# A small-tile feed-forward tail on one core: rounding moved from GpSimd to ScalarE, and the VectorE queue reordered

## The chip, the cores and the metric

One core of a Trainium2 chip runs the kernel. The metric is the device time of one execution in microseconds (us); the median of several is compared. Five queues run side by side and meet only in semaphores: TensorE (PE), VectorE (DVE), ScalarE (ACT), GpSimd (POOL) and SyncE (SP), which here only starts transfers.

## The reference

One layer over x of 16 x 64 rows of 256: cross-attention on a context, a state-space block (Mamba), and a quantised feed-forward block, which the change is about. Cut to that block:

```python
def _act_quant(x):
    scale = 127.0 / jnp.clip(jnp.max(jnp.abs(x), axis=-1, keepdims=True), 1e-05)
    return jnp.clip(jnp.round(x * scale), -128.0, 127.0) / scale
def _bitlinear(x, w):
    return jnp.einsum('bsi,oi->bso', _act_quant(x), _weight_quant(w))
gate = jax.nn.silu(_bitlinear(xn, w_gate))      # 256 -> 1024
up = _bitlinear(xn, w_up)
x = x + _bitlinear(gate * up, w_down)           # 1024 -> 256, xn = layernorm(x)
```

## The kernel before

The 1024 rows are 8 tiles of 128 rows. Three stages follow one another: attention (to about 190 us), the scan of the state-space block (to about 360 us), and the feed-forward tail. Each engine has one queue, written out by hand; an instruction waits for semaphores (`wait_ge`) and whatever stands behind it waits too.

**The scan** is cut into 64 halves `hu`. For each, PE writes the inflow into PSUM, DVE scans it (`scan`, L1601, into a ring of 4 buffers), POOL multiplies by C (`weigh`, L1897, `g_ready`), and PE turns and adds it (`accumulate`, L759). `weigh(hu)` needs `scan(hu)`, and `scan(hu)` needs `weigh(hu - 4)`. Between the halves stand pieces of the tail for the first tiles: on DVE the statistics (`ffn_statistics`, L1659 and L1662, after halves 50, 52, 60 and 61) and the scale of a row (`input_scale`: reduce L1675, L1677, reciprocal L1679, and for the tiles 0 to 2 also L1681, which writes two scales for gate and up; after halves 54 and 56, and for tile 2 behind the last scan); on POOL `offset_input` (L1912, L1914, L1921) after halves 48, 50 and 60, and `rounded_to_bf16` (L1938) after halves 54 and 56.

**The tail**, for each tile t: normalise the row (ACT L1123 for tiles 0 to 2, POOL L1932 else), largest magnitude and its inverse (`input_scale`), scale and round by adding a large number (ACT L1130 or POOL L1965, `hi`), subtract it again and write bf16 (POOL L1938, `input_to_bf16`, `f_hq`), transpose on PE (L790), copy to SBUF (ACT L1221, `copy_input`), gate and up matmuls (L801, L812), SiLU (ACT L1302), product in DVE (`product`, L1688), its largest magnitude (`largest`, L1693), `inner_scale` (L1705, L1707, L1709), scale and round (ACT L1309, `round_inner`), back to bf16 (DVE L1716, `inner_to_bf16`), transpose (L824), copy (ACT L1317, `copy_inner`), down matmul (L837), output (DVE L1724), store. Only tile 7 does the inner part in two halves.

The second half of the state-space output, tiles 4 to 7, is still being made while tiles 0 to 3 are in the tail: `gate(7)` (DVE L1610) needs the last `accumulate`; then PE turns four blocks (L770), ACT copies them (`copy_yz`, L1215), PE multiplies them (`out_proj_of`, L778) and DVE adds them to the residual (`add_scan(1, 0)` and `add_scan(1, 1)`, L1649), after which the statistics of tiles 4, 5 and 6, 7 can be taken. The order of the DVE queue in the middle of the tail is

```python
product(2); largest(2); inner_scale(2); inner_to_bf16(1)
add_scan(1, 0); ffn_statistics(4); ffn_statistics(5); inner_to_bf16(2); input_scale(4); product(3)
```

and that of ACT there is `round_inner(1)`, `round_inner(2)`, `copy_input(3, 4)`, `copy_yz(1, 2, 2)`, `copy_inner(0)`, `silu_gate(3)`. PE has after `out_proj_of(1, 1, 3)`: `turn_input(3, 4)`, `turn_gated(1, 2, 2)`, `activations(0)`, `gates(3)`, `turn_gated(1, 3, 2)`, `up(3)`, `activations(1)`, then `out_proj_of` for the last two tiles.

Of the kernel before, what the change touches and what calls it, by code (L numbers as in the profile page):

```python
# [17 lines left out]
ALU = mybir.AluOpType  # L18
# [6 lines left out]
P = 128  # L25
# [4 lines left out]
NT = B * L // P  # L30
# [76 lines left out]
def build(nc, x, ctx_t, mask, wq, wkv, wproj, bproj, vecs, cons, win, wall, wout, wg, wu, wd, out):  # L107
    with ExitStack() as ctx:
# [106 lines left out]
        f_s2 = [sb(f"f_s2{t}", [P, 5]) for t in range(NT)]  # L215
        f_nmean = sb("f_nmean", [P, NT_ACT])
        C_M2, C_CL2, C_INV2, C_A, C_OUT = range(5)

# [109 lines left out]
        f_inv, f_sgs = sem("f_inv", DVE), sem("f_sgs", DVE)  # L328
        f_hi_ready, f_hq = sem("f_hi_ready", POOL), sem("f_hq", POOL)
# [4 lines left out]
        f_a, f_os, f_gi_ready = sem("f_a", DVE), sem("f_os", POOL), sem("f_gi_ready", ACTE)  # L334
        f_gq, f_gqt, f_gqt_sb = sem("f_gq", DVE), sem("f_gqt", PE), sem("f_gqt_sb", ACTE)
        f_down, f_out = sem("f_down", PE), sem("f_out", DVE)
        stored = [sem("stored0", SP), sem("stored1", SP)]
# [142 lines left out]
        def _(pe):  # L480
# [346 lines left out]
            def down(t):  # L827

                if t == 0:
                    pe.wait_ge(yz_sb, count(NG * GT))  # L830
                if t == 3:
                    pe.wait_ge(x2_ready, count(NT))
                pe.wait_ge(f_out, count(t if t < 3 else t - 1))
                for n, cols in enumerate(inner_parts(t)):
                    pe.wait_ge(f_gqt_sb, count(t + 1 + n))
# [153 lines left out]
        def _(act):  # L989
# [216 lines left out]
            def copy_yz(g, tt, k):  # L1206
# [8 lines left out]
                act.activation(yz[:, tt % 2], bank(k), ACT.Copy).then_inc(yz_sb, 1)  # L1215

            def copy_input(t, k):
# [71 lines left out]
            round_input(0)  # L1289
            slot(15)  # L1290
            round_input(1)
            copy_input(0, SPARE_BANK)
            copy_input(1, SPARE_BANK)
            normal_input(2)
# [9 lines left out]
            def round_inner(t):  # L1304

                act.wait_ge(f_a, count(t + 1))
                act.wait_ge(f_gq, count(t - 1))
                for cols in inner_parts(t):
                    act.activation(f_gi[t % 2][:, cols], f_gu[t % 2][:, cols], ACT.Copy,  # L1309
                                   scale=f_s2[t][:, C_A:C_A + 1], bias=MAGIC).then_inc(f_gi_ready, 1)  # L1310

            def copy_inner(t):

                act.wait_ge(f_down, count(t - 1))
                for n, cols in enumerate(inner_parts(t)):
# [9 lines left out]
            silu_gate(1)  # L1325
            round_inner(0)
# [10 lines left out]
            copy_yz(1, 3, 2)  # L1337
            copy_inner(1)
            round_inner(3)
            copy_input(4, 4)  # L1340
            silu_gate(4)
            copy_inner(2)
            copy_input(5, 4)
            copy_inner(3)
            silu_gate(5)
            round_inner(4)
            copy_input(6, 4)
            silu_gate(6)
            round_inner(5)
# [11 lines left out]
        def _(dve):  # L1361
# [334 lines left out]
            def inner_scale(t):  # L1696

                s2, up_scale = f_s2[t], f_s[t][:, C_SU:C_SU + 1]

                def col(c):  # L1700
                    return s2[:, c:c + 1]

                dve.wait_ge(f_max2, count(t + 1))
                dve.wait_ge(*weights_scaled(t))
                dve.tensor_scalar(col(C_CL2), col(C_M2), up_scale, EPS, ALU.mult, ALU.max).then_inc(f_cl2, 1)  # L1705
                dve.wait_ge(f_cl2, count(t + 1))
                dve.reciprocal(col(C_INV2), col(C_CL2)).then_inc(f_inv2, 1)  # L1707
                dve.wait_ge(f_inv2, count(t + 1))
# [112 lines left out]
        def _(pool):  # L1821
# [112 lines left out]

            def input_to_bf16(t):

                pool.wait_ge(f_hqt, count(t - 1))
                pool.tensor_scalar(f_hqb[t % 2], f_hi[t % 2], MAGIC, 127.0, ALU.subtract, ALU.min).then_inc(f_hq, 1)  # L1938

            def scale_weights_of(t):  # L1940
# [6 lines left out]
            def scale_output(t):  # L1947

                s2 = f_s2[t]
                pool.wait_ge(f_cl2, count(t + 1))  # L1950
                pool.tensor_scalar(s2[:, C_OUT:C_OUT + 1], s2[:, C_CL2:C_CL2 + 1], wmean[:, 2:3], 1.0 / 127.0, ALU.mult,
                                   ALU.mult).then_inc(f_os, 1)

            def rounded_to_bf16(t):

                if t == 0:
                    pool.wait_ge(delta_ready, count(NG * NC))
                pool.wait_ge(f_hi_act, count(t + 1))
                input_to_bf16(t)

            def round_input(t):

                pool.wait_ge(f_inv, count(t + 1))
                pool.wait_ge(f_hq, count(t - 1))
                pool.tensor_scalar(f_hi[t % 2], f_h[t % 2], f_s[t][:, C_INV:C_INV + 1], MAGIC, ALU.mult, ALU.add  # L1965
                                   ).then_inc(f_hi_ready, 1)
                pool.wait_ge(f_hi_ready, count(t - NT_ACT + 1))
                input_to_bf16(t)

# [14 lines left out]
            for hu in range(NHU - 1):  # L1984
# [25 lines left out]
            scale_weights_of(5)  # L2010
            scale_output(3)
            normal_input(6)
            normal_input(7)
            round_input(6)
            scale_weights_of(6)
# [62 lines left out]
```

## Time and profile before

| what | value |
|---|---|
| median of 3 runs | 410.5 us (409.54 to 410.86) |
| profiled execution, its own time | 412.68 us |
| its span, first to last instruction | 410.8 us |
| busy share of the span: PE, DVE, ACT, POOL | 88%, 85%, 68%, 69% |
| mean granted TensorE clock | 0.992 |

The page gives the busy time of each engine, the chain of work that ended last, and groups of instructions by line. Some 1.9 us of the profiled execution lie outside its span. The tail, which the change touches, is the stretch from about 340 us on.

### The profile page before, as it was taken

How to read it: one execution, taken by the hardware profiler on the slowest of the kernel's cores; microseconds unless marked ns; L12 is line 12 of the kernel's file. 1: busy time of each engine (PE TensorE's matmuls, PEld its weight loads, DVE VectorE, ACT ScalarE, POOL GpSimd, SP SyncE). 2: the span in 40 equal slices, each digit the busy share in tenths (PEclk: the TensorE clock that was granted, in tenths of full speed). 3: DMA queues.
4: the chain of work that ended last, by engine and by line, in shares of the span. 5: the costliest groups of instructions: out<-in, count | busy, mean ns of one | idle time of the engine just before them, and what ended most of it. 6: DMA issues, size and time to landing. Idle time of an engine off the chain costs nothing.

```text
span 410.8 us, 8698 instructions
## 1 busy us (share of the span) xinstructions
PE 361.4 (88%) x2886; PEld 246.2 (60%) x2886; DVE 348.2 (85%) x723; ACT 278.7 (68%) x596; POOL 285.5 (69%) x333
## 2 busy tenths in 40 slices
PE   7899999999998999887798999898889778889774
PEld 5556767676776765453465566566576656557442
DVE  1558888797989778958989999989999999988795
ACT  1267589769966993489569879857874554266574
POOL 0056475565657472248999999999999699986830
PEclk9999999999999999999699999999999999999999
DMA  7981010110100000019400001364000000000001
GB/s 209 357 360 53 2 51 14 42 51 3 53 2 0 2 3 0 2 38 249 128 2 0 2 4 26 92 191 129 2 1 2 1 2 0 2 0 2 14 26 65
DMA packets 23039, 22.41 MB, mean 55 GB/s; under 512 B 1074, under 2 KB 20914, under 8 KB 22484
## 3 DMA queue, kind: packets, MB, share of 16 engines
q1 hardware_dynamic: 22436, 21.39, 16.7%
q8 instruction: 23, 0.38, 0.4%
q10 hardware_dynamic: 560, 0.48, 0.4%
q14 instruction: 20, 0.16, 0.1%
HBM read 20.75 MB, written 1.12 MB: 53 GB/s over the span
## 4 chain that ended last, share of the span: by engine, by line
PE 28%; DVE 20%; ACT 17%; POOL 17%; issue 16%; DMA 1%; DVEq 0%; PEld 0%; POOLq 0%; SPq 0%; ACTq 0%; PEldq 0%
POOL both L1897 12%; PE ps L544 7%; ACT both L1181 5%; DVE both L1601 4%; PE ps L513 4%; PE ps L496 3%; DVE both L1425 2%; PE ps L531 2%; PE ps L607 2%; PE ps L574 2%; ACT both L1016 2%; PE ps L759 2%; PE ps L561 2%; DVE f_s L1693 1%; ACT both L1167 1%
## 5 line engine op out<-in xcount | busy, mean ns | idle before, releaser
L1897 POOL TENSOR_TENSOR both<-both 128x1024 f32<-128x1024 f32 x64 | 150.4, 2386 | 2.4 <-DVE both L1601 1.8
L1601 DVE TENSOR_TENSOR_SCAN both<-both,ps 128x1024 f32<-128x1024 f32 x64 | 143.0, 2271 | 5.6 <-PE ps L749 5.5
L1843 POOL TENSOR_SCALAR both<-both,rden 128x256 f32<-128x256 f32 x128 | 61.7, 497 | 62.8 <-DVE rden L1432 62.6
L1181 ACT ACTIVATE both<-delta,a_neg 128x504 f32<-128x504 f32 x120 | 74.8, 704 | 12.3 <-DVE both L1601 12.2
L759 PE MATMUL ps<-con,both 128*128 128x128 f32 x512 | 72.5, 281 | 7.5 <-POOL both L1897 7.4
L759 PEld LDWEIGHTS ps<-con,both 128*128 128x128 f32 x512 | 56.8, 142 | 29.5 <-issue 16.3
L1016 ACT ACTIVATE both<-both,negmax 128x256 f32<-128x256 f32 x128 | 63.3, 498 | 15.7 <-DVE negmax L1425 15.7
L749 PE MATMUL ps<-both 32*128 32x256 f32 x512 | 46.7, 435 | 11.7 <-DVE both L1601 9.6
L1425 DVE CUSTOM_DVE_ANT_0 both<-ps,both 128x256 f32<-128x256 f32 x128 | 46.9, 417 | 6.7 <-PE ps L496 5.5
L513 PEld LDWEIGHTS ps<-con,both 128*128 128x128 f32 x256 | 30.6, 141 | 12.7 <-issue 8.0
L513 PE MATMUL ps<-con,both 128*128 128x128 f32 x256 | 38.2, 275 | 0.0
L749 PEld LDWEIGHTS ps<-both 32*128 32x128 f32 x512 | 20.5, 186 | 27.6 <-DVE both L1601 15.5
L544 PE MATMUL ps<-both 128*128 128x512 f32 x64 | 33.0, 640 | 2.7 <-DMA both<-in_wkv 1.3
L574 PE MATMUL ps<-both 128*128 128x256 f32 x128 | 31.1, 387 | 0.5 <-DVE both L1400 0.5
L1437 DVE COPY both<-ps 128x512 f32<-128x512 f32 x32 | 21.6, 676 | 10.2 <-PE ps L513 10.2
L1022 ACT ACTIVATE both<-ps 128x512 f32<-128x512 f32 x32 | 18.8, 588 | 14.6 <-PE ps L513 14.6
L574 PEld LDWEIGHTS ps<-both 128*128 128x128 f32 x128 | 23.1, 190 | 6.0 <-issue 2.7
L1016 ACT ACTIVATION_READ_ACCUMULATOR both<-both,negmax 128x1 f32 x128 | 24.5, 191 | 0.0
L1826 POOL TENSOR_TENSOR vareps<-meanvar,eps 128x1 f32<-128x1 f32 x24 | 6.3, 261 | 25.5 <-DVE meanvar L1377 25.5
L496 PE MATMUL ps<-both 32*128 32x256 f32 x256 | 20.6, 399 | 3.0 <-DVE negmax L1425 2.0
L544 PEld LDWEIGHTS ps<-both 128*128 128x128 f32 x64 | 11.3, 197 | 14.9 <-issue 13.0
L496 PEld LDWEIGHTS ps<-both 32*128 32x128 f32 x256 | 13.2, 184 | 8.3 <-issue 6.7
(151 smaller groups left out, 616.7 us busy)
## 6 DMA issues: line engine op xcount, KB each, us to landing
both<-bounce SPq DMA_DIRECT2D x16, 512.0 KB, 6.4
both<-in_ctx_t SPq DMA_DIRECT2D x8, 512.0 KB, 3.4
both<-in_wg SPq DMA_DIRECT2D x1, 1024.0 KB, 8.9
both<-in_wu SPq DMA_DIRECT2D x1, 1024.0 KB, 10.6
both<-in_wd SPq DMA_DIRECT2D x1, 1024.0 KB, 12.6
win_sb<-in_win SPq DMA_DIRECT2D x1, 1024.0 KB, 13.8
resid<-in_x SPq DMA_DIRECT2D x1, 896.0 KB, 6.3
both<-in_wkv SPq DMA_DIRECT2D x2, 256.0 KB, 3.4
```

What stands on the lines that cost most here:

```text
L496: mm = pe.matmul(score_bank(tile, v)[:, bb * LK:(bb + 1) * LK], q2[rows, tile.par, hf, bb].rearrange("p r q -> p (r q)"), kt_sb[rows, tile ...
L513: tr = pe.transpose(pt_bank(tile, u)[:, (q * 2 + kt) * P:(q * 2 + kt + 1) * P], sm[:, u, q * LK + kt * P:q * LK + (kt + 1) * P], ident)
L544: mm = pe.matmul(kv_bank(tile, hf), wkv_sb[:, k, hf * P:(hf + 1) * P], ctx_sb[:, tile.par, k], start=k == 0, stop=k == KD - 1)
L574: mm = pe.matmul(kv_bank(tile, 1 - bb)[:, kt * D:(kt + 1) * D], ctx_sb[:, tile.par, k, bb * LK + kt * P:bb * LK + (kt + 1) * P], wkv_sb[:, ...
L749: mm = pe.matmul(bank(inflow_bank(hu) + sq).rearrange("p (n h t) -> p n h t", n=HN, h=2)[:, :, th], ut[rows, e.idx % 2, tt], bd[rows, e.nh ...
L759: mm = pe.matmul(bank(Y_BANK)[:, e.tt * P:(e.tt + 1) * P], g_sb[:, hu % RING_G, n * P:(n + 1) * P], ident, start=False, stop=e.nh == NH - ...
L1016: act.activation(s, s, ACT.Exp, scale=-1.0, bias=negmax[:, u, q:q + 1], accum_out=den[:, u, q:q + 1]).then_inc(expd, 1)
L1181: act.activation(da[sl % 2].rearrange("p (a s n t) -> p a s n t", a=GT, n=HN, s=2)[:, :, :, n, 1:L], delta[:, idx % RING_D].rearrange("p ( ...
L1425: dve.tensor_tensor_reduce(sm[:, u, q * LK:(q + 1) * LK], score_bank(tile, u)[:, q * LK:(q + 1) * LK], maskf[:, tile.par, q * LK:(q + 1) * ...
L1601: dve.tensor_tensor_scan(h_sb[:, hu % RING_H], da[e.slot % 2][:, e.tt * HU:(e.tt + 1) * HU], bank(inflow_bank(hu), 2), 0.0, ALU.mult, ALU. ...
L1843: pool.tensor_scalar(s, s, rden[:, u, q:q + 1], 1.0, ALU.mult, ALU.mult).then_inc(normed, 1)
L1897: pool.tensor_tensor(g_sb[:, hu % RING_G].rearrange("p (n s t) -> p s n t", n=HN, s=2), h_sb[:, hu % RING_H].rearrange("p (s n t) -> p s n ...
```

## The change

Six edits. (1) `input_to_bf16` goes from POOL (subtract and minimum in one operation) to ACT (an activation that adds minus the large number), placed in ACT's queue by hand, the first one in the middle of the last block of decays. With that `rounded_to_bf16` leaves POOL. (2) `product` multiplies by the up scale too (`scalar_tensor_tensor` in place of `tensor_tensor`), so that `inner_scale` needs two small operations and no longer L1709. (3) A one-column SiLU on ACT stands ahead of the first real one, so that the table is loaded there. (4) In the DVE queue `add_scan(1, 0)` and the statistics of 4 and 5 stand ahead of `inner_scale(2)` and `inner_to_bf16(1)`; `input_scale(4)` stands ahead of `inner_to_bf16(2)`; the statistics of 7 ahead of `inner_to_bf16(3)` and `output(0)`. On POOL `scale_output(3)` stands behind two normalisations. (5) At the end `largest(7)` and `inner_scale(7)` stand ahead of `inner_to_bf16(6)`, that of 7 ahead of `output(5)`, and on ACT `round_inner(7)` ahead of `copy_inner(6)`. (6) The second half of the last `copy_inner` is made by DVE (`copy_last_half`).

```diff
+            def input_to_bf16(t):
+                if t < NT_ACT:
+                    act.wait_ge(f_hi_act, count(t + 1))
+                else:
+                    act.wait_ge(f_hi_ready, count(t - NT_ACT + 1))
+                act.wait_ge(f_hqt, count(t - 1))
+                act.activation(f_hqb[t % 2], f_hi[t % 2], ACT.Copy, bias=-MAGIC).then_inc(f_hq, 1)
...
-            slot(15)
+            half_slot(15, 0)
+            input_to_bf16(0)
+            half_slot(15, 1)
             round_input(1)
             copy_input(0, SPARE_BANK)
+            input_to_bf16(1)
             copy_input(1, SPARE_BANK)
             normal_input(2)
...
+            act.activation(f_warm[:], eps[:], ACT.Silu).then_inc(passed, 1)
             act.wait_ge(y_seed, count(NG * NC))
...
             round_inner(1)
+            input_to_bf16(3)
             round_inner(2)
...
+            round_inner(7)
             copy_inner(6)
-            round_inner(7)
             copy_inner(7)
...
-                dve.tensor_tensor(f_gu[t % 2], bank(0, 2), f_sg[t % 2], ALU.mult).then_inc(f_gu_ready, 1)
+                dve.wait_ge(*weights_scaled(t))
+                dve.scalar_tensor_tensor(f_gu[t % 2], bank(0, 2), f_s[t][:, C_SU:C_SU + 1], f_sg[t % 2], ALU.mult, ALU.mult
+                                         ).then_inc(f_gu_ready, 1)
...
-                dve.tensor_scalar(col(C_A), col(C_INV2), up_scale, 127.0, ALU.mult, ALU.mult).then_inc(f_a, 1)
...
+            def copy_last_half():
+                t = NT - 1
+                cols = inner_parts(t)[1]
+                dve.wait_ge(f_gqt, count(t + 2))
+                dve.wait_ge(f_down, count(t - 1))
+                dve.tensor_copy(f_gqtb[t % 2].rearrange("p k t -> p (k t)")[:, cols], f_inner(1)[:, cols]
+                                ).then_inc(f_last_half, 1)
...
             largest(2)
-            inner_scale(2)
-            inner_to_bf16(1)
             add_scan(1, 0)
             ffn_statistics(4)
             ffn_statistics(5)
+            inner_scale(2)
+            inner_to_bf16(1)
+            input_scale(4)
             inner_to_bf16(2)
-            input_scale(4)
             product(3)
...
             ffn_statistics(6)
+            ffn_statistics(7)
             inner_to_bf16(3)
             output(0)
-            ffn_statistics(7)
...
             product(7)
-            inner_to_bf16(6)
             largest(7)
             inner_scale(7)
+            inner_to_bf16(6)
             output(4)
+            inner_to_bf16(7)
             output(5)
-            inner_to_bf16(7)
+            copy_last_half()
...
-                if hu in (54, 56):
-                    rounded_to_bf16((54, 56).index(hu))
             weigh(NHU - 1)
-            rounded_to_bf16(2)
```

## Rows read from the trace of the kernel before

**Rows 1.** The chain that ended last, in order of time: start us, us, what.

```profile
360.04 4.69 POOL both L1897 x2
364.77 1.10 PE ps L759 x8
...
385.76 1.23 POOL xnt L1932
```

**Rows 2.** Timeline of POOL, end of the scan: start us, us, engine, line, operation.

```profile
330.89 9.30 POOL L1897 TENSOR_TENSOR both<-both 128x1024 f32<-128x1024 f32 x4
340.28 1.07 POOL L1938 TENSOR_SCALAR dtb<-xnt 128x256 bf16<-128x256 f32 x1
357.74 6.98 POOL L1897 TENSOR_TENSOR both<-both 128x1024 f32<-128x1024 f32 x3
```

**Rows 3.** Timeline of DVE, end of the scan and start of the tail.

```profile
334.12 1.47 DVE L1681 TENSOR_SCALAR f_s<-wmean,f_s 128x2 f32<-128x2 f32 x1
340.56 0.21 DVE L1681 TENSOR_SCALAR f_s<-wmean,f_s 128x2 f32<-128x2 f32 x1
348.47 2.28 DVE L1601 TENSOR_TENSOR_SCAN both<-both,ps 128x1024 f32<-128x1024 f32 x1
354.22 4.46 DVE L1601 TENSOR_TENSOR_SCAN both<-both,ps 128x1024 f32<-128x1024 f32 x2
359.30 0.81 DVE L1681 TENSOR_SCALAR f_s<-wmean,f_s 128x2 f32<-128x2 f32 x1
361.22 1.23 DVE L1688 TENSOR_TENSOR zst<-ps,xc 128x1024 f32<-128x1024 f32 x1 [1.11 <-ACT xc L1302]
366.51 1.21 DVE L1693 TENSOR_REDUCE f_s<-zst 128x1 f32<-128x1024 f32 x1
```

**Rows 4.** Line L1622, its two forms: durations min/median/max in ns.

```profile
L1622 DVE TENSOR_TENSOR u_sb<-xc,delta x4: 661/686/1710, 182.1 to 198.0; 128x512 f32<-128x512 f32 x4
L1622 DVE TENSOR_TENSOR u_sb<-ps,delta x4: 662/665/665, 266.4 to 319.8; 128x512 f32<-128x512 f32 x4
```

**Rows 5.** Timeline of DVE, middle of the tail.

```profile
373.36 0.75 DVE L1649 TENSOR_TENSOR resid<-ps,resid 128x256 f32<-128x256 f32 x2
378.18 1.23 DVE L1688 TENSOR_TENSOR zst<-ps,xc 128x1024 f32<-128x1024 f32 x1
387.01 0.42 DVE L1675 TENSOR_REDUCE f_s<-xnt 128x1 f32<-128x256 f32 x1 [1.94 <-POOL xnt L1932]
400.01 1.22 DVE L1688 TENSOR_TENSOR zst<-ps,xc 128x1024 f32<-128x1024 f32 x1
```

**Rows 6.** Groups by line and shape: busy us, mean ns, idle before.

```profile
L1716 DVE TENSOR_SCALAR both<-delta 128x1024 bf16<-128x1024 f32 x7 | 4.8, 687 | 0.0
L1938 POOL TENSOR_SCALAR dtb<-xnt 128x256 bf16<-128x256 f32 x6 | 6.9, 1147 | 0.5
L1709 DVE TENSOR_SCALAR f_s<-f_s 128x1 f32<-128x1 f32 x8 | 1.7, 214 | 0.3
L1130 ACT ACTIVATE xnt<-xnt,f_s 128x256 f32<-128x256 f32 x1 | 0.5, 497 | 0.0
L1557 DVE SCALAR_TENSOR_TENSOR xc<-ps,vec,xc 128x496 f32<-128x496 f32 x4 | 2.9, 720 | 1.6 <-ACT zst L1114 1.6
```

**Rows 7.** Timeline of ACT, start, middle and end of the tail.

```profile
358.78 1.28 ACT L1302 ACT_TABLE_LOAD   x1 [0.37 <-PE ps L801]
372.88 1.15 ACT L1309 ACTIVATE delta<-zst,f_s 128x1024 f32<-128x1024 f32 x1 [1.98 <-DVE f_s L1709]
406.37 1.08 ACT L1317 ACTIVATE both<-ps 128x512 bf16<-128x512 bf16 x2 [0.55 <-PE ps L824]
```

**Rows 8.** Timeline of PE, middle of the tail.

```profile
369.41 3.62 PE L778 MATMUL ps<-wout_sb,yz 128*128 128x256 f32 x16
374.36 1.04 PE L801 MATMUL ps<-wgq,dtb 128*128 128x512 bf16 x4 [0.33 <-ACT dtb L1221]
```

**Rows 9.** The last output, timeline of DVE.

```profile
408.18 0.48 DVE L1724 SCALAR_TENSOR_TENSOR z<-ps,f_s,resid 128x256 f32<-128x256 f32 x1 [1.51 <-PE ps L837]
```

More of the change, by code:

```diff
@@ L216, in build @@
         f_nmean = sb("f_nmean", [P, NT_ACT])
+        f_warm = sb("f_warm", [P, 1])
         C_M2, C_CL2, C_INV2, C_A, C_OUT = range(5)
@@ L328, in build @@
         f_inv, f_sgs = sem("f_inv", DVE), sem("f_sgs", DVE)
-        f_hi_ready, f_hq = sem("f_hi_ready", POOL), sem("f_hq", POOL)
+        f_hi_ready, f_hq = sem("f_hi_ready", POOL), sem("f_hq", ACTE)
         f_hqt, f_hqt_sb = sem("f_hqt", PE), sem("f_hqt_sb", ACTE)
@@ L333, in build @@
         f_gu_ready, f_cl2, f_inv2 = sem("f_gu_ready", DVE), sem("f_cl2", DVE), sem("f_inv2", DVE)
-        f_a, f_os, f_gi_ready = sem("f_a", DVE), sem("f_os", POOL), sem("f_gi_ready", ACTE)
+        f_os, f_gi_ready = sem("f_os", POOL), sem("f_gi_ready", ACTE)
         f_gq, f_gqt, f_gqt_sb = sem("f_gq", DVE), sem("f_gqt", PE), sem("f_gqt_sb", ACTE)
+        f_last_half = sem("f_last_half", DVE)
         f_down, f_out = sem("f_down", PE), sem("f_out", DVE)
@@ L834, in down @@
                 for n, cols in enumerate(inner_parts(t)):
-                    pe.wait_ge(f_gqt_sb, count(t + 1 + n))
+                    if n:
+                        pe.wait_ge(f_last_half, count(1))
+                    else:
+                        pe.wait_ge(f_gqt_sb, count(t + 1))
                     for j in range(cols.start // P, cols.stop // P):
@@ L1215, in copy_yz @@
                 act.activation(yz[:, tt % 2], bank(k), ACT.Copy).then_inc(yz_sb, 1)
+            def input_to_bf16(t):
+                if t < NT_ACT:
+                    act.wait_ge(f_hi_act, count(t + 1))
+                else:
+                    act.wait_ge(f_hi_ready, count(t - NT_ACT + 1))
+                act.wait_ge(f_hqt, count(t - 1))
+                act.activation(f_hqb[t % 2], f_hi[t % 2], ACT.Copy, bias=-MAGIC).then_inc(f_hq, 1)
             def copy_input(t, k):
@@ L1304, in round_inner @@
             def round_inner(t):
-                act.wait_ge(f_a, count(t + 1))
+                act.wait_ge(f_inv2, count(t + 1))
                 act.wait_ge(f_gq, count(t - 1))
@@ L1309, in round_inner @@
                     act.activation(f_gi[t % 2][:, cols], f_gu[t % 2][:, cols], ACT.Copy,
-                                   scale=f_s2[t][:, C_A:C_A + 1], bias=MAGIC).then_inc(f_gi_ready, 1)
+                                   scale=f_s2[t][:, C_INV2:C_INV2 + 1], bias=MAGIC).then_inc(f_gi_ready, 1)
             def copy_inner(t):
                 act.wait_ge(f_down, count(t - 1))
-                for n, cols in enumerate(inner_parts(t)):
+                for n, cols in enumerate(inner_parts(t)[0:1]):
                     act.wait_ge(f_gqt, count(t + 1 + n))
@@ L1325, in _ @@
             silu_gate(1)
+            input_to_bf16(2)
             round_inner(0)
@@ L1338, in _ @@
             copy_inner(1)
+            input_to_bf16(4)
             round_inner(3)
             copy_input(4, 4)
+            input_to_bf16(5)
             silu_gate(4)
@@ L1345, in _ @@
             silu_gate(5)
+            input_to_bf16(6)
             round_inner(4)
             copy_input(6, 4)
+            input_to_bf16(7)
             silu_gate(6)
@@ L1696, in inner_scale @@
             def inner_scale(t):
-                s2, up_scale = f_s2[t], f_s[t][:, C_SU:C_SU + 1]
-                def col(c):
-                    return s2[:, c:c + 1]
+                s2 = f_s2[t]
                 dve.wait_ge(f_max2, count(t + 1))
-                dve.wait_ge(*weights_scaled(t))
-                dve.tensor_scalar(col(C_CL2), col(C_M2), up_scale, EPS, ALU.mult, ALU.max).then_inc(f_cl2, 1)
+                dve.tensor_scalar(s2[:, C_CL2:C_CL2 + 1], s2[:, C_M2:C_M2 + 1], EPS, 1.0 / 127.0, ALU.max, ALU.mult
+                                  ).then_inc(f_cl2, 1)
                 dve.wait_ge(f_cl2, count(t + 1))
-                dve.reciprocal(col(C_INV2), col(C_CL2)).then_inc(f_inv2, 1)
-                dve.wait_ge(f_inv2, count(t + 1))
-                dve.tensor_scalar(col(C_A), col(C_INV2), up_scale, 127.0, ALU.mult, ALU.mult).then_inc(f_a, 1)
+                dve.reciprocal(s2[:, C_INV2:C_INV2 + 1], s2[:, C_CL2:C_CL2 + 1]).then_inc(f_inv2, 1)
             def inner_to_bf16(t):
@@ L1933, in normal_input @@
                                    ALU.mult).then_inc(f_xn, 1)
-            def input_to_bf16(t):
-                pool.wait_ge(f_hqt, count(t - 1))
-                pool.tensor_scalar(f_hqb[t % 2], f_hi[t % 2], MAGIC, 127.0, ALU.subtract, ALU.min).then_inc(f_hq, 1)
             def scale_weights_of(t):
@@ L1950, in scale_output @@
                 pool.wait_ge(f_cl2, count(t + 1))
-                pool.tensor_scalar(s2[:, C_OUT:C_OUT + 1], s2[:, C_CL2:C_CL2 + 1], wmean[:, 2:3], 1.0 / 127.0, ALU.mult,
+                pool.tensor_scalar(s2[:, C_OUT:C_OUT + 1], s2[:, C_CL2:C_CL2 + 1], wmean[:, 2:3], 1.0, ALU.mult,
                                    ALU.mult).then_inc(f_os, 1)
[L1954 to L1959, printed above, removed]
             def round_input(t):
@@ L1966, in round_input @@
                                    ).then_inc(f_hi_ready, 1)
-                pool.wait_ge(f_hi_ready, count(t - NT_ACT + 1))
-                input_to_bf16(t)
             pool.wait_ge(s_ready, count(NT * 8))
@@ L2010, in _ @@
             scale_weights_of(5)
-            scale_output(3)
             normal_input(6)
             normal_input(7)
+            scale_output(3)
             round_input(6)
```

## The prediction

> **What bounds the kernel now.** I read the page first: DVE is busy for 85% of the span, PE for 88%, POOL for 69%, so no share alone decides, and the change touches nothing before 340 us. So I read the chain of waits from there on. Up to 364.7 us it is POOL, one multiplication after the other; then PE turns the last one, and from there the chain runs through DVE, with POOL's normalisations between them [rows 1]. The timelines say how tight each queue is. POOL runs its 64 multiplications at 9.30 / 4 = 2.33 us each, and at 340.28 one conversion to bf16 of 1.07 us stands between them [rows 2]. DVE is just as full: none of its rows up to 360.11 has idle time before it, and a scan takes 2.28 us [rows 3]. Both engines set the pace, so time taken from POOL shows only where DVE does not need it itself.
>
> The row to look at longest is L1681, two columns wide. It took 1.47, 0.21 and 0.81 us [rows 3]. The long ones end at 335.59 and 360.11; POOL's multiplications end at 330.89 + 2 x 2.325 = 335.54 and at 357.74 + 2.33 = 360.07 [rows 2]. The short one ran inside POOL's bf16 conversion (340.28 to 341.35). So L1681 waits for the end of a two-input POOL multiplication that is already running, and not for the conversion. L1622 says the same from another side: with both inputs in SBUF one of four took 1710 ns against a median of 686, with one in PSUM all four took 662 to 665 [rows 4]. One-column operations (L1677, L1709 at 214 ns) show no such wait [rows 6].
>
> **Part by part: the end of the scan.** The change takes the conversion out of POOL at 340.28. The next multiplication then starts there and runs to 342.61. L1681 of tile 1 comes at 340.56, which is now inside it. It ends some 0.05 us behind it as in the two long cases, at 342.65 instead of 340.77: DVE +1.9 us, and with it every scan from there. This phase is no accident of one run: the first L1681 waited for POOL's end at 335.54 and so tied DVE to POOL; two scans, the reduce and two small ones later DVE is at 340.56, and two multiplications later POOL is at 340.2.
>
> POOL, relieved of 2 x 1.15 us, now waits for DVE. Before, scan 60 ended at 348.47 + 2.28 = 350.75 [rows 3]; now at 352.6. Multiplication 60 follows at once; three of them and the 1.15 us of `offset_input` later, number 63 starts at 352.65 + 3 x 2.33 + 1.15 = 360.8 and ends at 363.1 (before: 357.74 + 6.98 = 364.72 [rows 2]). From scan 60's end to L1681 of tile 2 it took 359.30 - 350.75 = 8.55 us, so it now comes at 361.15, again inside a multiplication, and ends at 363.15. The product of tile 0 starts there. Before it started at 361.22, held for 1.11 us by SiLU [rows 3], whose wait is gone now, since the gates need only multiplication 60. So the tail starts 1.9 us late on DVE although POOL ends 1.6 us early.
>
> The Trainium skill (SBUF — State Buffer, Who interferes with whom) calls the port pair that VectorE and GpSimd share an exclusive lock, held for a whole instruction, that a two-port `tensor_scalar` or a two-input VectorE operation needs. The two long L1681 and the long L1622 agree; that the one at 340.56 ran through a POOL conversion in 0.21 us does not.
>
> **Product and scales.** `scalar_tensor_tensor` is not in the trace at this size: with PSUM and 496 columns it took 720 ns, and scaled by the product's slope (1.23 us at 1024) a 1024-column one lies between 1.23 (no extra) and 1.49 us (720 x 1024 / 496). I take 1.29: most of the 720 is fixed and per-column time, and the product's own row is nearest in size. L1709 goes: 0.22 us of DVE from one start to the next. Net -0.16 us for each tile, bounds -0.22 and +0.04. From product(0) to largest(1) DVE took 5.29 us before, of which PE's wait was a part; now 2.89 for tile 0, 1.20 and 0.60 for product(1) and `gate(7)`, 4.7 in all: largest(1) at 367.8, +1.3 against 366.51 [rows 3].
>
> **The middle.** `add_scan(1, 0)` needs the first two output projections. They ended at 369.41 + 3.62 = 373.03 [rows 8]; they hang on `gate(7)`, also 1.3 us late (ready 367.9, not 366.6), so they end at 374.1 to 374.3. DVE gets there at 373.3 (product(2) +1.1) and waits; behind it stand two adds (0.7) and two statistics (1.2), and only then `inner_scale(2)`, done at 376.5. Before, ACT's `round_inner(2)` started at 372.88 [rows 7]; now at 376.5, +3.6. On ACT `copy_input(3)` stands behind it, for it wait the gates of tile 3 (374.36 before [rows 8], about 378.0 now), and behind them in PE's queue the fourth turn, up(3), and the last two projections. Not all of it arrives: before, product(3) at 378.18 [rows 5] was itself held by POOL's normalisation of tile 4; now SiLU(3) holds it to 380.4, +2.2. `add_scan(1, 1)` is also 2.2 late. Here POOL's relief pays: before, two conversions and three small operations stood ahead of `normal_input(6)` (385.76 [rows 1]); now POOL is free when the statistics come. The reduce of tile 6 was held 1.94 us by it, to 387.01 [rows 5]; I get 388.2 and product(4) at 389.1, +1.3 to +1.5. Were the old order of these lines kept, gates(3) would come at 375.3, and the end about 1.7 us sooner. So this reorder costs 1.7, and what it should bring, early statistics, is bounded by the projections, which it makes late itself.
>
> The moved conversions cost ACT about 0.4 each (256 columns with a pointer scale took 497 ns [rows 6]; bounds 0.4 to 0.5) and they lie in ACT's waits, 1.98 us at one place alone [rows 7]; 0.6 each would move nothing, and if that cover went it would be 0.4 us a tile. The early table load puts 1.28 us [rows 7] ahead of gates that now end earlier; DVE is at L1681 until 363.15, so it is worth nothing either way here (up to -1.1 if DVE were early). `scale_output(3)` and the statistics of 7: nothing, output(0) is not waited for before down(3).
>
> **Tiles 4 to 7.** From product(4) on DVE has no idle time until product(7) at 400.01 [rows 5]. Three tiles at -0.16 give -0.5: +0.9 there.
>
> **The end.** From product(7) to the last output it took 8.17 us [rows 5, 9]. The largest magnitude and its scale now come first, so bf16(6) starts 2.9 us behind product(7) and not 1.1. After it: 0.69, then turn 6 (0.6), copy 6 (1.0), down 6, half a turn of tile 7, half a copy (0.6), the last down. With the waits between them that is 5.9, 8.8 in all: +0.6. DVE's copy of the second half saves ACT about half of 1.08 us [rows 7], but DVE makes it beside the first half and down needs the first; whether it takes 0.42 or 0.68 the end stands.
>
> **Sum.** +1.9 (two port waits, SiLU's wait gone) - 0.6 (product(0) to largest(1)) + 0.9 (middle: +1.3 to +2.2) - 0.8 (POOL free for tile 6) - 0.5 (three tiles) + 0.6 (end) = +1.5 us, on a span of 410.8 and a profiled time of 412.68. The median lies 2.2 below that profiled one; I carry the difference over: 410.5 + 1.5 = 412.0. Worked through queue by queue with these durations the kernel before comes out 0.5 us short at product(7); with as much again for the steps that no row shows, +0.7 to +2.3 is this case's own range: 411.2 to 412.8.
>
> **The rivals.** What a measurement of this kernel can tell from no change is about 0.3%, 1.2 us.
>
> *The port waits do not come* (faster). If L1681 finds POOL between two instructions or the conversion on ACT changes their phase, nothing is lost at 340.56 and 361.15. Product(0) then starts at 359.3 (multiplication 60 ends at 353.1, and behind it lie one turn, the gates, a table load and SiLU, 4.5 us in all), and is 1.9 early instead of 1.9 late; the middle gives back 1.7, the rest brings what is said above: -2.6, 407.9 us. For it speaks that L1681 at 340.56 would meet POOL only 0.3 us behind an instruction's start; against it the three rows and the fixed phase. It decides as soon as L1681 of tile 1 takes under 0.6 us and that of tile 2 as well. Chance 0.2.
>
> *Only one of the two comes* (about no change). With the first gone POOL is 1.8 us ahead of DVE and number 63 starts at 358.95, so L1681 at 359.30 waits to 361.3: the same product(0) as before, -0.3 in all. With the second gone, -0.8. 409.7 to 410.2 us. Chance 0.18.
>
> *The queues slip further* (slower still). If `scalar_tensor_tensor` costs 1.49 and DVE, the fullest engine, waits for a late POOL at tile 6 as before, it is 5 x 0.2 + 0.8 more: 413.8 us. Chance 0.1.
>
> My forecast, both waits and the late middle: 0.52.
>
> **How the numbers follow.** The forecast's range is split by +1.2 us: a third of it lies below. Slower: two thirds of 0.52 and 0.1, 0.44. Same: one third of 0.52 and most of 0.18, 0.32. Faster: 0.2 and a rest of the middle case, 0.24. The range leaves out half of the fast case and most of the slowest: 408.0 to 413.2.
>
> **What would show it.** In the profile of the changed kernel L1681's successor should have one instance of about 2.1 us at 340.6 and another of 2.0 at 361.1; product(0) at 363.1; DVE idle before `add_scan(1, 0)` for 0.8; ACT idle before `round_inner(2)` for some 4 us; gates(3) at 378; 8.8 us from product(7) to the last output. I am wrong if the two L1681 are short, if gates(3) come before 376, or if the product with its scale takes much over 1.3 us.

## The result

The changed kernel takes 417.9 us (median of 4 runs, 417.6 to 418.7); the kernel before took 410.7 (4 runs, 409.5 to 412.8). The ratio is 1.0173, with a 95% interval of 1.014 to 1.0206: 7.2 us slower. The forecast was 412.0 us in a range of 408.0 to 413.2, so its sign holds and its size does not. The profiled execution took 417.61 us with a span of 415.8, and the mean granted clock of TensorE is 0.975, where it was 0.992.

**The two port waits came.** The timeline of DVE in the changed kernel, L1705 being what L1681 was (start us, us, engine, line, operation, and in brackets the idle time before it with its releaser):

```profile
338.66 1.99 DVE L1705 TENSOR_SCALAR f_s<-wmean,f_s 128x2 f32<-128x2 f32 x1
...
359.17 1.99 DVE L1705 TENSOR_SCALAR f_s<-wmean,f_s 128x2 f32<-128x2 f32 x1
361.08 1.27 DVE L1713 SCALAR_TENSOR_TENSOR zst<-ps,f_s,xc 128x1024 f32<-128x1024 f32 x1
...
372.81 0.76 DVE L1673 TENSOR_TENSOR resid<-ps,resid 128x256 f32<-128x256 f32 x2 [1.30 <-PE ps L780]
...
381.15 1.28 DVE L1713 SCALAR_TENSOR_TENSOR zst<-ps,f_s,xc 128x1024 f32<-128x1024 f32 x1 [2.88 <-PE ps L814]
...
402.39 1.27 DVE L1713 SCALAR_TENSOR_TENSOR zst<-ps,f_s,xc 128x1024 f32<-128x1024 f32 x1
...
410.89 0.43 DVE L1745 COPY both<-ps 128x512 bf16<-128x512 bf16 x1 [3.37 <-PE ps L826]
...
413.17 0.48 DVE L1753 SCALAR_TENSOR_TENSOR z<-ps,f_s,resid 128x256 f32<-128x256 f32 x1 [1.46 <-PE ps L842]
```

And POOL's there:

```profile
335.92 11.65 POOL L1927 TENSOR_TENSOR both<-both 128x1024 f32<-128x1024 f32 x5
347.87 2.36 POOL L1927 TENSOR_TENSOR both<-both 128x1024 f32<-128x1024 f32 x1 [0.29 <-DVE both L1625]
350.70 2.35 POOL L1927 TENSOR_TENSOR both<-both 128x1024 f32<-128x1024 f32 x1 [0.48 <-DVE both L1625]
...
354.16 6.99 POOL L1927 TENSOR_TENSOR both<-both 128x1024 f32<-128x1024 f32 x3
```

The second multiplication of the first row ends at 335.92 + 2 x 2.33 = 340.58 and L1705 at 340.65; the last one of the tail ends at 361.15 and L1705 at 361.16. Where the kernel before had 0.21 and 0.81 us [rows 3] there are now twice 1.99, and POOL, relieved of its conversions, waits for DVE (0.29 and 0.48).

**Then PE stops for 3.3 us, and comes back at half its clock.** ACT and PE in the middle and at the end:

```profile
354.86 1.28 ACT L1337 ACT_TABLE_LOAD   x1
375.13 1.15 ACT L1326 ACTIVATE delta<-zst,f_s 128x1024 f32<-128x1024 f32 x1 [4.62 <-DVE f_s L1729]
```

```profile
362.41 1.04 PE L814 MATMUL ps<-wuq,dtb 128*128 128x512 bf16 x4 [2.32 <-DVE zst L1713]
...
372.72 0.61 PE L826 MATMUL ps<-identb,both 128*128 128x128 bf16 x8
376.61 1.89 PE L803 MATMUL ps<-wgq,dtb 128*128 128x512 bf16 x4 [3.28 <-ACT dtb L1235]
378.29 1.06 PE L772 MATMUL ps<-con,zst 128*128 128x128 f32 x4
379.14 1.91 PE L814 MATMUL ps<-wuq,dtb 128*128 128x512 bf16 x4
...
404.10 1.03 PE L842 MATMUL ps<-wdq,both 128*128 128x256 bf16 x8 [1.27 <-ACT both L1334]
406.06 0.81 PE L826 MATMUL ps<-identb,both 128*128 128x128 bf16 x8 [0.94 <-DVE both L1736]
408.14 1.86 PE L842 MATMUL ps<-wdq,both 128*128 128x256 bf16 x8 [1.27 <-ACT both L1334]
...
411.27 1.87 PE L842 MATMUL ps<-wdq,both 128*128 128x256 bf16 x8 [0.41 <-ACT both L1334]
```

Windows of 2 us of the same kernel (busy time and count of PE, weight loads, DVE, ACT, POOL; then the granted clock, the DMA share and GB/s):

```profile
372.00:374.00 2.00, 1.33 (x16) 1.02 (x14) 1.09 (x3) 0.00 (x0) 0.00 (x0) 1.00 0.01 4
374.00:376.00 2.00, 0.00 (x0) 0.00 (x0) 1.50 (x6) 0.86 (x1) 1.50 (x3) 0.90 0.00 0
376.00:378.00 2.00, 1.39 (x4) 0.57 (x5) 1.08 (x4) 1.96 (x4) 1.81 (x4) 0.50 0.00 0
378.00:380.00 2.00, 2.00 (x9) 1.19 (x7) 0.27 (x1) 1.46 (x2) 2.00 (x3) 0.50 0.00 0
...
382.00:384.00 2.00, 2.00 (x9) 1.73 (x9) 1.90 (x5) 1.33 (x2) 0.00 (x0) 0.89 0.00 0
...
408.00:410.00 2.00, 1.86 (x10) 1.37 (x11) 0.00 (x0) 0.00 (x0) 0.00 (x0) 0.50 0.19 66
410.00:412.00 2.00, 1.59 (x13) 1.17 (x11) 0.82 (x2) 0.60 (x1) 0.00 (x0) 0.50 0.00 0
```

The column to read is the granted clock, 1.00 being 2.4 GHz and 0.50 being 1.2 GHz. The four gate matmuls of tile 3 took 1.04 us before [rows 8] and take 1.89 now, up(3) 1.91, and DVE waits 2.88 us for it. At the end the last two groups of down matmuls take 1.86 and 1.87 instead of 1.03. In the kernel before every such window from 366 to 410 us shows 1.00; its stretches at half clock lie between 190 and 210 us.

The table counts the us in each trace from the start of the two-column operation of tile 1 (340.56 before, 338.66 after). Absolute times would mislead: between 200 and 210 us DVE is busy for 8.04 us in the profiled run before and for 10.00 in the one after, and what lies behind is shifted by about as much. The last two columns are differences to before.

| start of | before | forecast | after |
|---|---|---|---|
| product(0) | 20.66 | +1.9 | +1.76 |
| gates(3) | 33.80 | +3.6 | +4.15 |
| product(3) | 37.62 | +2.2 | +4.87 |
| product(4) (387.76 before) | 47.20 | +1.3 to +1.5 | +4.88 |
| product(7) | 59.45 | +0.9 | +4.28 |
| last output | 67.62 | +1.5 | +6.89 |

The 6.9 us of this table are the 7.2 of the medians to 0.3. Up to gates(3) the forecast follows to 0.6 us; at product(3) the kernel is 2.7 us later than forecast, and behind product(7) it loses 2 more.

### The profile page after: what moved, and what is told of

It reads as the page before. It is cut to its first block, busy times and chain, and to the rows that moved or that the text cites. A ratio compares the mean times of both kernels' runs of the same rounds, so it can differ in the third digit from the quotient of the medians.

```text
span 415.8 us, 8688 instructions
## 1 busy us (share of the span) xinstructions
PE 365.5 (88%) x2882; PEld 248.8 (60%) x2886; DVE 349.9 (84%) x716; ACT 281.4 (68%) x604; POOL 279.1 (67%) x325
## 4 chain that ended last, share of the span: by engine, by line
PE 34%; DVE 26%; issue 14%; ACT 13%; POOL 10%; DMA 1%; DVEq 1%; PEld 0%; SPq 0%; ACTq 0%; POOLq 0%; PEldq 0%
DVE both L1625 8%; PE ps L546 7%; POOL both L1927 6%; ACT both L1186 5%; PE ps L515 4%; PE ps L498 3%; PE ps L761 2%; PE ps L533 2%; PE ps L780 2%; PE ps L751 2%; DVE both L1449 2%; PE ps L576 2%; ACT both L1021 2%; PE ps L563 2%; DVE f_s L1719 1%
## 5 line engine op out<-in xcount | busy, mean ns | idle before, releaser
L761 PE MATMUL ps<-con,both 128*128 128x128 f32 x512 | 71.2, 278 | 3.2 <-POOL both L1927 3.2
L515 PEld LDWEIGHTS ps<-con,both 128*128 128x128 f32 x256 | 30.6, 141 | 12.7 <-issue 8.0
L515 PE MATMUL ps<-con,both 128*128 128x128 f32 x256 | 38.2, 275 | 0.0
```

The costliest lines, as they stand in the source:

```text
L515: tr = pe.transpose(pt_bank(tile, u)[:, (q * 2 + kt) * P:(q * 2 + kt + 1) * P], sm[:, u, q * LK + kt * P:q * LK + (kt + 1) * P], ident)
L761: mm = pe.matmul(bank(Y_BANK)[:, e.tt * P:(e.tt + 1) * P], g_sb[:, hu % RING_G, n * P:(n + 1) * P], ident, start=False, stop=e.nh == NH - ...
```

## The experiments

Times are medians; ratios, with their 95% intervals, are to the kernel before on the same chip. Four kernels (all three, and the three parts put into the kernel before) ran on another chip than the others; the kernel before took 411.2 us there and 410.7 here, so a difference of medians across the two can be off by some 0.5 us. The ratios on record can differ from the quotient of two medians by up to 0.3%. In the expectations theory A is the account that the profile after suggests: port waits, a late middle, and a clock that falls in PE's gap; its rivals put the time elsewhere. Where matmuls are added, they write a bank that nobody reads.

**The old order in the middle of the DVE queue**, all else as after:

```diff
             largest(2)
+            inner_scale(2)
+            inner_to_bf16(1)
             add_scan(1, 0)
             ffn_statistics(4)
             ffn_statistics(5)
-            inner_scale(2)
-            inner_to_bf16(1)
-            input_scale(4)
             inner_to_bf16(2)
+            input_scale(4)
```

> The changed kernel with the old order in the middle of the DVE queue (inner_scale(2) and inner_to_bf16(1) ahead of add_scan(1, 0), inner_to_bf16(2) ahead of input_scale(4)). Theory A (the late inner_scale(2) starves PE for 3.3 us, its clock falls to half, and gates(3), up(3) and what lies between run at half speed): PE's gap ahead of gates(3) under 1.5 us, gates(3) 1.04 us and not 1.89, granted clock 1.0 from 374 to 390, 1.7 us for the order and some 3.0 us for the clock, so 413.2 us; the slow clock at the end stays. Theory B (queue order alone, the clock falls whatever the gap): 1.7 us, so 416.2, gates(3) still 1.9 us. The two port waits of 1.99 us stay in both.

411.7 us (10 runs), ratio 1.0002 (0.997 to 1.0035): the order gives back 6.2 us, more than either theory said. Gates(3) start without a gap, at full clock. But the profiled run also had a full clock at the end (8.71 us from product(7) to the last output, not 10.78), and half clock elsewhere, behind the gap ahead of up(1). In the trace this is -4.1 us between product(0) and product(7) and -2.1 behind it. The reorder alone thus did not separate the middle from the clock of the end. The window with that gap in this kernel:

```profile
358.00:364.00 6.00, 3.69 (x16) 2.37 (x15) 5.36 (x6) 2.45 (x3) 3.25 (x4) 0.72 0.00 0
```

**Two one-column scales** in place of the two-column one, all else as after:

```diff
-dve.tensor_scalar(col(C_SG, 2), wmean[:, 0:2], col(C_CL), None, ALU.mult).then_inc(f_sgs, 1)
+dve.tensor_scalar(col(C_SG), wmean[:, 0:1], col(C_CL), None, ALU.mult).then_inc(passed, 1)
+dve.tensor_scalar(col(C_SU), wmean[:, 1:2], col(C_CL), None, ALU.mult).then_inc(f_sgs, 1)
```

> The changed kernel with the two-column scaling of tiles 0 to 2 written as two one-column operations. Theory A (a two-column operation needs both ports and waits for POOL's running multiplication, a one-column one does not): no DVE operation of that line over 0.25 us, product(0) some 3.5 to 3.9 us behind nothing, that is about 1.9 us earlier each for tiles 1 and 2 less 0.2 for the added operation, limited by the gates to about 2.5; the end earlier by 2 to 3.5: 414.5 to 416. Theory B (the DVE waits were hidden behind SiLU and the projections): under 0.5 us, 417.5.

411.5 us (10 runs), ratio 1.0 (0.9976 to 1.0025): 6.4 us less than the changed kernel, again more than expected. Each one-column operation takes 0.20 us beside POOL's running multiplications, and product(0) comes 4.0 us sooner, counted from the scales of tile 0 (24.86 us against 28.87), since that tile's wait of 1.47 goes too. Product(0) to product(7) gains 1.25 and the end 0.9: PE is at half clock for less of both (up(3) takes 1.50 and not 1.91, the last two groups of down matmuls 1.32 and 1.72). The middle gap is still there:

```profile
371.15 1.87 PE L803 MATMUL ps<-wgq,dtb 128*128 128x512 bf16 x4 [2.90 <-ACT dtb L1235]
373.67 1.50 PE L814 MATMUL ps<-wuq,dtb 128*128 128x512 bf16 x4
```

**PE kept busy in the middle gap**, with all waits left in:

```diff
+def warm(t, n):
+    pe.wait_ge(f_silu, count(t))
+    for _ in range(n):
+        pe.matmul(bank(6), identb[:], wgq[:, 0, 0:512], start=True, stop=True)
...
+            warm(3, 14)
             gates(3)
```

> The changed kernel with 14 more matmuls of 512 columns into a free bank ahead of the wait of gates(3), so that PE has no gap there; nothing else is moved. Theory A (half clock because of the gap): gates(3), up(3), the turn and two thirds of the last projections run at full clock, 0.85 + 0.45 + 0.87 + 0.45 + 0.4 = 3.0 us less, 414.9 us, ACT's wait for inner_scale(2) unchanged at 4.6. Theory B (the clock is not what is lost): no change or up to 0.3 slower, 418.

413.4 us (10 runs, 412.7 to 417.5), ratio 1.0069 (1.0035 to 1.0103): 4.5 us won by adding work, 1.5 more than expected.

```profile
362.36 1.04 PE L819 MATMUL ps<-wuq,dtb 128*128 128x512 bf16 x4 [2.33 <-DVE zst L1719]
...
373.11 3.19 PE L798 MATMUL ps<-wgq,identb 128*128 128x512 bf16 x14
376.55 1.04 PE L808 MATMUL ps<-wgq,dtb 128*128 128x512 bf16 x4 [0.25 <-ACT dtb L1241]
```

Gates(3) start when they did (37.94 us behind the scales of tile 1, after: 37.95) but take 1.04, and product(3) is 2.1 us earlier, product(7) 2.8. In this run the end had full clock as well (8.71 us from product(7) to the last output), without any edit to it, which the expectation had not counted. The ten runs have mean clocks of 0.975 to 0.996, so the clock fell in more places in some of them than in this one.

**PE kept busy at the end only**: `warm(8, 4)` ahead of the down matmuls of tile 5, the activations of tile 6 and its down matmuls.

> The changed kernel with 4 more matmuls of 512 columns ahead of each of down(5), activations(6) and down(6), into a bank that SiLU(7) has left. Theory A (the clock falls at the end because PE has more and longer gaps there than before): down(6) 1.04 and not 1.86 us, down(7) 1.04 and not 1.87, turns 0.85 and not 1.06: 0.8 + 0.2 + 0.9 less, about 416.0 us. Theory B (the end is late by its queue order alone, 0.6): 417.9. Cost if the added matmuls delay the real ones: up to 0.4.

416.8 us (4 runs), ratio 1.0134 (1.0093 to 1.0175). The end takes 8.71 us and all its down matmuls 1.03, 2.1 less than after; the middle is as in after. The time falls by only 1.0, for two reasons. In the profiled run another place lost its clock, one that had it in after and in the run above, behind a gap of the same length; that costs 0.7 us by product(7):

```profile
362.39 1.86 PE L819 MATMUL ps<-wuq,dtb 128*128 128x512 bf16 x4 [2.32 <-DVE zst L1721]
...
377.40 1.89 PE L808 MATMUL ps<-wgq,dtb 128*128 128x512 bf16 x4 [3.28 <-ACT dtb L1243]
```

And two of the four runs took 3.5 and 3.6 us outside their span, from first to last instruction, where the kernels without added matmuls take 1.8 to 1.9; why is not known. The spans themselves are 413.7 to 414.4 us against 415.8 to 416.9 in the changed kernel, some 2.1 less by their medians, which is what the end gives.

**PE kept busy in all three gaps**: nine matmuls ahead of up(1), behind a wait for the last scan, then 14 and 3 x 4 as above.

> The changed kernel, its queues as they are, with added matmuls into free banks in all the long gaps of PE: 9 ahead of up(1), 14 ahead of gates(3), 4 each ahead of down(5), activations(6) and down(6). Theory A (the time above the forecast of 412.0 is TensorE's half clock and nothing else): granted clock 1.0 from 352 us on, 412 to 413 us, 5 us under the changed kernel. Theory B (half of it is something else, not seen yet): 414.5 or more.

412.7 us (12 runs, 411.0 to 415.6), ratio 1.0051 (1.0023 to 1.008). The windows and the DVE timeline:

```profile
350.00:366.00 16.00, 12.90 (x94) 8.54 (x95) 15.53 (x19) 6.71 (x10) 12.33 (x11) 1.00 0.00 0
366.00:384.00 18.00, 17.75 (x108) 12.71 (x109) 13.49 (x32) 10.91 (x16) 7.52 (x15) 1.00 0.00 1
...
398.00:412.00 14.00, 8.66 (x71) 5.39 (x69) 7.68 (x17) 5.80 (x7) 1.54 (x2) 1.00 0.13 47
```

```profile
359.10 1.99 DVE L1717 TENSOR_SCALAR f_s<-wmean,f_s 128x2 f32<-128x2 f32 x1
...
372.73 0.76 DVE L1685 TENSOR_TENSOR resid<-ps,resid 128x256 f32<-128x256 f32 x2 [1.30 <-PE ps L780]
...
399.48 1.27 DVE L1725 SCALAR_TENSOR_TENSOR zst<-ps,f_s,xc 128x1024 f32<-128x1024 f32 x1
...
408.19 0.48 DVE L1765 SCALAR_TENSOR_TENSOR z<-ps,f_s,resid 128x256 f32<-128x256 f32 x1 [0.83 <-PE ps L847]
```

Both port waits of 1.99 us and DVE's 1.30 us ahead of the first `add_scan` are still in it; only the clock differs, 1.00 throughout from 330 us to the last output. The clock therefore cost the changed kernel about 5 us: 5.1 by the medians (417.86 - 412.72), 4.9 from the scales of tile 1 to the last output in the traces, 5.3 by the medians of the spans. What lies ahead does not enter: the changed kernel's profiled run has a clock of 0.66 between 190 and 200 us and this run 1.00, and yet the scales of tile 0 start at 332.21 and 332.15. Not every run had the full clock (means of 0.987 to 1.0). This kernel is what the forecast described, and it stands 0.7 us from it; even product(3) is held by SiLU (0.77 us), as forecast, and no longer by up(3).

**The old orders of the middle and of the end**, the two-column scales kept. The end's edit is

```diff
             product(7)
+            inner_to_bf16(6)
             largest(7)
             inner_scale(7)
-            inner_to_bf16(6)
             output(4)
-            inner_to_bf16(7)
             output(5)
+            inner_to_bf16(7)
...
-            round_inner(7)
             copy_inner(6)
+            round_inner(7)
```

> The changed kernel with both old orders and the two-column scales kept, so that the port waits alone are left of the three losses. Theory A: two waits of 2.0 us, 3.7 us later than e7_all_three at product(0), 409.5, a little under the kernel before; the clock falls in some runs in the 2.3 us gap ahead of up(1), which adds up to 2 us. Theory B (with the middle mended the port waits are covered): 406.

410.3 us (12 runs), ratio 0.9989 (0.9963 to 1.0015), as expected (409.5, and up to 2 more where the clock falls). PE's gap in the middle is gone, and at the end its gaps are those of the kernel before but for 0.3 us (1.26, 1.26 and 0.38, at full clock). The port waits still leave one ahead of up(1), behind which the clock is half for part of the time:

```profile
364.13 1.43 PE L814 MATMUL ps<-wuq,dtb 128*128 128x512 bf16 x4 [2.31 <-DVE zst L1713]
```

**One-column scales and the old middle**, with the new end kept:

> The changed kernel with one-column scales and the old order in the middle, the new order at the end kept. Against e7_all_three it tells what the new end costs. Theory A: 8.7 us from product(7) to the last output against 7.9 in e7, so 405.9 and up to 1 us more where the clock falls in the longer gaps. Theory B (the end order is neutral): 405.1.

408.2 us (8 runs), ratio 0.9912 (0.9883 to 0.9941), above the 405.9 to 406.9 expected. It lies 3.0 above the next kernel, which ran on the other chip and from which it differs in the end alone; counted from the scales of tile 0 the traces differ by 2.8. Its end takes 10.68 us, at half clock:

```profile
400.00:406.00 6.00, 3.76 (x21) 2.41 (x19) 1.30 (x3) 0.60 (x1) 0.00 (x0) 0.50 0.12 44
```

The eight runs fall into two groups: five with mean clocks of 0.984 to 0.987 and spans of 406.3 to 406.9 us, three with 0.995 to 1.0 and 404.6 to 405.1. The same program thus loses some 1.7 us or not, as its clock falls or not.

**All three**: one-column scales, old middle, old end; the conversions on ACT, the scaled product, the early table and DVE's half copy stay.

> The changed kernel with all three put back or mended: one-column scales, the old order in the middle of the DVE queue, and the old order at the end (inner_to_bf16(6) ahead of largest(7), copy_inner(6) ahead of round_inner(7) on ACT). Theory A (what the change brings is real, POOL relieved and one small operation less a tile, and was covered by the three losses): product(0) 2 to 3 us earlier against the last scan than before, no idle time ahead of the first add_scan, 8.2 us from product(7) to the last output and not 8.7: 406 to 408 us, faster than before. Theory B (the gain was never there): 410.7, like before. Clock drops that come in some runs may add 1 to 2 us.

405.1 us (6 runs), ratio 0.9854 (0.9821 to 0.9887), under the 406 to 408 expected: faster than both kernels, than the one before by 6.1 us on the same chip and than the changed one by 12.7 us across chips. The granted clock is 1.00 in every window from 330 us to the last output. Its end, on DVE:

```profile
394.61 1.27 DVE L1714 SCALAR_TENSOR_TENSOR zst<-ps,f_s,xc 128x1024 f32<-128x1024 f32 x1
395.80 0.68 DVE L1737 TENSOR_SCALAR both<-delta 128x1024 bf16<-128x1024 f32 x1
...
402.49 0.48 DVE L1754 SCALAR_TENSOR_TENSOR z<-ps,f_s,resid 128x256 f32<-128x256 f32 x1 [0.59 <-PE ps L842]
```

From product(7) to the last output it takes 7.88 us; bf16(6) starts 1.2 behind product(7). At full clock the new order takes 8.71: the order itself costs 0.8 us, and the clock, where it falls, 2.0 on top.

Last, parts of the change put into the kernel before. **One-column scales alone**:

> The kernel before with the one-column scales alone. Its two waits for POOL (1.26 and 0.6 us) go. Theory A: POOL's queue sets the end of the scan there and SiLU holds product(0), so little comes of it: 410.0 to 410.7. If DVE were what binds there, 409.

411.0 us (10 runs), ratio 0.9999 (0.9973 to 1.0025). Nothing: product(0) comes 27.11 us behind the scales of tile 0, before 27.10. DVE no longer waits for POOL, but it waits longer for SiLU ahead of product(0), 1.64 us where it was 1.11 [rows 3], so its port waits had cost nothing there:

```profile
357.72 1.23 DVE L1689 TENSOR_TENSOR zst<-ps,xc 128x1024 f32<-128x1024 f32 x1 [1.64 <-ACT xc L1302]
```

**The conversions on ACT alone** (edit 1), and **that with one-column scales**:

> The kernel before with one part of the change alone: the conversions to bf16 made by ACT at the places where the change puts them; no new order on DVE, no product with scale, no early table. Theory A: two waits of 2.0 us for POOL's running multiplication on DVE, so product(0) 1.8 us later against the second scale than before, POOL's relief gives back 0.8 to 1: 411.5, plus 1 to 2 us where the clock falls in the gap of 2.3 us ahead of up(1). Theory B (POOL was the bound and is relieved of 3.4 us before the tail): 408 to 409.

> As e9_before_act_only, with one-column scales, so that DVE has no wait for POOL's multiplications. Theory A: product(0) 3.7 us earlier than in e9 against the scans, the end 3 us earlier than e9 and 2 to 3 us earlier than before: 407.5 to 408.7. Theory B (the port waits were hidden): as e9.

410.3 us (10 runs), ratio 0.9974 (0.9948 to 0.9999), and 406.8 us (4 runs), ratio 0.9899 (0.9861 to 0.9937), 0.7 under the range expected. Taking the conversions from POOL is enough to make both long waits, without any reorder:

```profile
338.56 1.99 DVE L1698 TENSOR_SCALAR f_s<-wmean,f_s 128x2 f32<-128x2 f32 x1
359.08 1.99 DVE L1698 TENSOR_SCALAR f_s<-wmean,f_s 128x2 f32<-128x2 f32 x1
```

Product(0) comes 28.87 us behind the scales of tile 0 with the waits and 24.84 without (before: 27.10). So the edit costs 1.8 us there as it was made, and brings 2.3 with one-column scales. The first kernel still came out 1.2 us lower than expected: between product(0) and product(7) it gains 1.4 us against before and at the end 0.3, where I had credited POOL's relief with 0.8. From the scales of tile 0 on this leaves it even with the kernel before (+0.1 us); the 0.9 us between the medians lie ahead of them or in the scatter. In the kernel before the one-column scales were worth nothing. Here they are worth 3.5 us, and as much in the changed kernel with the old middle (411.7 - 408.2); in the changed kernel itself 6.4, the clock included. With both old orders the medians of two chips say 5.2 (410.3 - 405.1), the traces 3.7. The prices of these edits do not add, because each one decides which wait the next one meets.

## Why the forecast was right in sign and wrong in size

**The port waits: right.** Forecast: two of 2.0 to 2.1 us and product(0) +1.9; measured 1.99, 1.99 and +1.76. That they wait for POOL's two-input multiplication follows from their ends (0.01 and 0.07 us behind POOL's) and from the one-column kernels, where nothing waits in the same places. The Trainium skill (SBUF — State Buffer, Who interferes with whom) calls the shared port pair an exclusive lock, and the rows of 1.98 to 2.00 us in seven kernels agree. That one column escapes it at 0.20 us is what these runs add.

**Product and scales: right.** 1.27 to 1.28 us at 1024 columns, taken as 1.29.

**The middle: the waits right, their price wrong.** DVE idles 1.30 us ahead of `add_scan(1, 0)` (forecast 0.8), ACT 4.6 ahead of `round_inner(2)` (forecast about 4), gates(3) come at +4.15 (forecast +3.6). The order's own cost, forecast 1.7, is 1.5 at full clock: product(0) to product(7) takes 38.47 us with PE kept busy in all gaps and 37.01 in the kernel with all three put back. The step that failed is the next one. "+0.9 (middle: +1.3 to +2.2)" counts what PE does behind the gap at the durations of [rows 8]. In the kernel at full clock throughout product(3) stands at +2.75, product(4) at +2.03 and product(7) at +1.44, against +2.2, +1.3 to +1.5 and +0.9: the waiting costs what the forecast said, to 0.7 us. In the changed kernel they stand at +4.87, +4.88 and +4.28. The missing 2.8 us are the half clock, in which gates(3), four turns, up(3), eight turns and the first part of the last projections ran; the sum has no term for it. Every piece needed to see it was in the prediction, projections that end at 374.1 to 374.3 and gates(3) at about 378.0, except the question at what clock PE comes back. (The measured gap is 373.3 to 376.6.) The kernel before, from whose rows every duration came, had no half clock in the tail of its profiled run.

**The end: the order right, its price wrong.** "+0.6 (end)": 8.8 us forecast, 8.71 measured at full clock, 10.78 in the changed kernel. The 2.1 us between are down(6), a turn and down(7) at half clock, behind gaps of 1.27, 0.94 and 1.27 us. The sum has no term for this either. The order's 8.71 us stand against 8.17 in the kernel before, as forecast, but against 7.88 with the old order in the changed kernel, so it costs 0.8 and not 0.6.

**The rest.** The conversions lie in ACT's waits and the table load moved to 354.86, without effect on product(0), as said; even with one-column scales product(0) comes 24.84 us behind the scales of tile 0 with the late load and 24.85 to 24.86 with the early one, where the forecast had allowed up to 1.1. DVE's copy takes 0.43 us. POOL's relief was sized low: 1.7 us and not 0.8 with the conversions alone moved.

**The rivals.** The first, that the port waits do not come, is refuted here and is true of the one-column kernels; its "1.9 early instead of 1.9 late" at product(0) was 2.2 to 2.3. Its 407.9 us is refuted too: the changed kernel without port waits took 411.5, since the gap in the middle stays at 2.90 us with half clock behind it. That only one wait comes is refuted by two of 1.99 us, and the slowest rival's product of 1.49 us by 1.27 to 1.28. The sign, given a chance of 0.44, was earned: without the clock the changed kernel would be about 0.5% or 2.0 us slower, more than the 1.2 us that the forecast called telling. That it is 1.7% slower comes from a cost that the forecast did not have.

**What stays open.** Which gaps lower the clock. The same 2.3 us ahead of up(1) left it at full in the profiles of the changed kernel and of the one with PE busy in the middle, and halved it in three others, wholly or in part, one of them the same program up to there as the changed kernel (PE busy at the end only); the end's gaps did so in some kernels and not in others, where nothing at the end was changed. That the added matmuls keep the clock up at the end thus rests on the spans of four runs more than on the one profile; in the middle it rests on the same gap with and without them. The 3.3 us of the middle, and the 2.9 of the one-column kernel, halved it each time they were profiled (three kernels). The 5.1 us is measured; which share of it falls to which gap in a given run is not, since only one execution of each kernel was profiled. The kernel before loses clock too: its 15 runs of 49 on the first chip with a clock of 1.00 have spans of 407.6 to 408.9 us, median 408.0, against 408.9 for all; the four such runs with PE busy in all gaps have 408.9 to 411.0. The medians also give the best kernel 1.5 us more than its trace does against after (-11.2 us from the scales of tile 0 on), and 1.8 more against before (6.1 and 4.3); the stretch ahead of them ends between 330.4 and 334.1 us in the profiled runs and was not studied.

## What to carry to other kernels

When an edit makes TensorE wait, price the wait twice: what comes later, and how long the next microseconds of matmuls last if they run at 1.2 GHz; here the clock cost 2.1 us at the product where the waits had cost 2.75, behind a gap of 3.3 us. Before work is taken off GpSimd, look at every VectorE operation that had been fitting between its instructions, and make the small ones one column wide. An edit that is worth nothing in the kernel before (one-column scales, ratio 0.9999) was worth 3.5 to 6.4 us once its neighbour had moved, so parts should be tried on the changed kernel and not only on the old one.

## What the runs showed of the hardware

- After the gap of 3.28 us PE's clock was at half for some 6 us: groups of four 512-column bf16 matmuls took 1.89 and 1.91 us instead of 1.04, eight turns 1.06 instead of 0.61. Matmuls of no use in the gap kept it at full. The Trainium skill (TensorE: Matmul & The Clock Gate, Part 1) tells of these two clock levels and that activity raises the clock; the rows agree, with a granted clock of 0.50 behind the gap and 1.00 where it was filled.
- Whether a gap of 2.3 us halves the clock differs between executions (1.04 against 1.86 us for the same four matmuls behind it).
- A `tensor_scalar` of 128x2 waits for POOL's running two-input operation (1.99 us), the same on 128x1 does not (0.20).
- What looks like the same lock was met from the other side too, though no run tests it. POOL's one-column `scale_output` takes 0.26 us; three times it started beside a conversion of DVE from fp32 to bf16 in SBUF (0.70 us), and took 0.77. The normalisation L1962 takes 1.22 us alone, and 1.56 and 1.64 where such a conversion ran:

```profile
377.73 1.64 POOL L1962 TENSOR_SCALAR xnt<-resid,f_s 128x256 f32<-128x256 f32 x1
...
380.05 0.26 POOL L1976 TENSOR_SCALAR f_s<-f_s,wmean 128x1 f32<-128x1 f32 x1
...
397.90 0.77 POOL L1976 TENSOR_SCALAR f_s<-f_s,wmean 128x1 f32<-128x1 f32 x1 [2.28 <-DVE f_s L1726]
```
